# Routed experts as three f16 products of split operands, with the weights as the loaded operand

## The reference: what is computed

```
logits = xt @ gate_w.T
_, idx = top_k(logits + beta, 2)
probs = sigmoid(take_along_axis(logits, idx))
g = einsum('bh,ehm->bem', xt, gate_proj_w)      # 8 experts, 256 -> 512
u = einsum('bh,ehm->bem', xt, up_proj_w)
h = silu(g) * u
eo = einsum('bem,emh->beh', h, down_proj_w)     # 512 -> 256
combined = einsum('beh,be->bh', eo, c)          # c: probs at the two chosen experts, else 0
shared_out = the same three products with one shared expert, for every token
```

## Time and profile before

| | |
|---|---|
| median of 3 runs | 3458.92 us |
| span of the profiled execution | 3454.1 us |
| what lies around the span, by the median | 4.8 us |
| granted TensorE clock, mean | 0.982 |
| phase 1 (8 blocks) | 0 to 308 us |
| phase 2 (72 tiles) | 308 to 758 us |
| the rest | 758 to 3454 us |

### The profile page before, as it was taken

One profiled execution on the slowest core, in us unless ns is written; L12 is line 12 of the kernel. 1 busy time (PEld: TensorE's weight loads), 2 busy tenths in 40 slices (PEclk: granted clock), 3 DMA queues, 4 the chain that ended last, 5 costly groups with the idle time before them and its releaser, 6 DMA issues. The chain is left out here.

```text
span 3454.1 us, 59006 instructions
## 1 busy us (share of the span) xinstructions
PE 3251.6 (94%) x19214; PEld 1316.3 (38%) x19215; DVE 2715.8 (79%) x4886; ACT 2222.3 (64%) x3468; POOL 1600.3 (46%) x2080
## 2 busy tenths in 40 slices
PE   8998999999999999999999999778999999999987
PEld 5655666652222222222222222252334334333333
DVE  5564222559999999999999999366989999898997
ACT  3331222127888888888878888757877777777763
POOL 2124000003444343344444443306888888887885
PEclk9999999999999999999999999988999999999998
DMA  4443111111121111111111110041222222222221
GB/s 156 133 163 114 47 45 44 42 42 30 35 60 41 39 38 33 31 32 31 34 36 35 35 36 23 30 141 59 71 74 69 82 73 69 74 83 69 76 77 50
DMA packets 160884, 211.56 MB, mean 61 GB/s; under 512 B 32324, under 2 KB 108364, under 8 KB 160604
## 3 DMA queue, kind: packets, MB, share of 16 engines
q1 hardware_dynamic: 141340, 172.51, 16.6%
q0 software_dynamic: 8512, 18.76, 1.7%
q10 hardware_dynamic: 10752, 16.78, 1.5%
HBM read 154.48 MB, written 52.69 MB: 60 GB/s over the span
## 5 line engine op out<-in xcount | busy, mean ns | idle before, releaser
L1289 ACT ACTIVATE prob<-psS 128x1024 f32<-128x1024 f32 (+3 forms) x1280 | 1104.1, 906 | 275.2 <-PE psS L1473 265.6
L1339 DVE TENSOR_REDUCE pmax<-psR 128x1 f32<-128x512 f32 x1674 | 1057.0, 684 | 76.9 <-PE psR L1415 46.6
L2115 POOL TENSOR_TENSOR hc<-h_d,crep 128x512 f32<-128x512 f32 x512 | 647.3, 1272 | 187.1 <-DVE h_d L2344 136.8
L1415 PE MATMUL psR<-kslab,qslab 48*128 48x512 bf16 (+3 forms) x2480 | 651.9, 351 | 22.2 <-DVE pmax L1339 13.8
L1488 PE MATMUL psVo<-prob,vaug 128*32 128x512 f32 (+3 forms) x5120 | 627.1, 543 | 1.7 <-ACT ov L1293 0.9
L1473 PE MATMUL psS<-qslab,kslab 51*128 51x512 bf16 (+3 forms) x2560 | 531.8, 352 | 39.5 <-ACT prob L1289 24.0
L2344 DVE TENSOR_TENSOR_SCAN h_d<-a,state,psU 128x512 f32<-128x512 f32 x384 | 489.4, 1275 | 0.0
L1204 POOL TENSOR_SCALAR_AFFINE_SELECT prob<-prob 128x256 f32<-128x256 f32 (+1 forms) x512 | 213.4, 420 | 529.0 <-ACT prob L1289 529.0
L1415 PEld LDWEIGHTS psR<-kslab,qslab 48*128 48x128 bf16 x2480 | 187.3, 94 | 627.9 <-DVE pmax L1339 468.7
L2334 DVE TENSOR_TENSOR psU<-dtx,psX 128x512 f32<-128x512 f32 x512 | 356.2, 696 | 88.9 <-PE psX L2494 38.5
L2247 ACT ACTIVATE a<-dt,a_neg 128x512 f32<-128x512 f32 x512 | 366.8, 724 | 53.8 <-DVE h_d L2344 53.0
(11 more groups left out here) (309 smaller groups left out, 4805.5 us busy)
## 6 DMA issues: line engine op xcount, KB each, us to landing
crep<-c_rows_d SPq DMA_DIRECT2D x256, 256.0 KB, 3.2
x_e<-rows_d SPq DMA_DIRECT2D x72, 128.0 KB, 2.0
y_d<-y SPq DMA_DIRECT2D x72, 128.0 KB, 1.7
q_d<-parts SPq DMA_DIRECT2D x48, 128.0 KB
k_d<-parts SPq DMA_DIRECT2D x48, 128.0 KB
qslab<-q_d SPq DMA_DIRECT2D x60, 96.0 KB
kslab<-k_d SPq DMA_DIRECT2D x60, 96.0 KB
x<-in_L_attn_x_dram SPq DMA_DIRECT2D x8, 512.0 KB, 6.3
```

The lines of the kernel that those rows point to most:

```text
L1289: act.activation(prob[g % BUFS][:, :, off:BLK], psS[g % 2][:, :, off:BLK], ACT.Exp).then_inc(prob_ready, 1)
L1339: dve.tensor_reduce(into[:, lo:lo + (count - 1) * NEXT + 1:NEXT], psR[at % BANKS][:, 0:count * w].rearrange("p (n w) -> p n w", w=w), AX.X ...
L1415: ins = pe.matmul(dst[:, m * w:(m + 1) * w], qslab[u][rows, i * P:(i + 1) * P], kslab[u][rows, ch * BLK:ch * BLK + w], start=(m == 0), sto ...
L2115: pool.tensor_tensor(hc[:, g % CR], h[:, g % HR], crep[:, g // PAIR % SPR], ALU.mult).then_inc(hc_ready, 1)
```

## The change: what it does

In phase 2 each f32 product becomes three f16 products. An operand is split into a high part (the f16 nearest to it) and a low part (the rest, in f16), and high x high, low x high and high x low are added up in PSUM. For g and u the roles are exchanged: the weights, in pieces of 128 x 128, are the loaded operand, and the 128 tokens stream. So g, u and h come out with the hidden dimension on the partitions, the four transposes of h go, and h is split directly. The last product has h's parts loaded and 256 columns of weights streaming. A tile has 48 matmuls of 128 columns and 12 of 256 in place of 4 of 512, 4 of 256 and 4 transposes. psG and psU have one buffer in place of two, and the maxima three banks in place of one.

f16 has a small range, so weights are scaled by their largest magnitude. In phase 1, for each expert: its three raw matrices are loaded into one buffer `raw`; DVE takes the maximum of magnitudes over 128 x 3072 numbers (`weight_max`); PE turns the maxima (`turn_max`), DVE reduces them (`weight_row`), PE spreads them (`spread_max`), DVE computes the scales (`weight_scale`); ACT writes the high part and scales `raw` in place (`high_weights`, `scaled_weights`, six operations of 128 x 1024), and POOL subtracts to the low part (`low_weights`, three operations). Factors that undo the scales go into the silu, the product with u and the routing weights. `raw` has one buffer, so the load of expert n+1 waits for the low parts of expert n. x is now loaded where it is normalized, and `cut` has four operations in place of five.

The diff, cut to its core:

```diff
@@ phase_norm_qkv, VectorE
-                c.after(dve.tensor_tensor(rest[:], qf[:, s], parts[:, s, 0], ALU.subtract))
-                c.after(dve.tensor_copy(parts[:, s, 1], rest[:]))
-                c.after(dve.tensor_tensor(rest[:], rest[:], parts[:, s, 1], ALU.subtract))
-                dve.tensor_copy(parts[:, s, 2], rest[:]).then_inc(parts_ready[s], 1)
+                c.after(dve.tensor_tensor(qf[:, s], qf[:, s], parts[:, s, 0], ALU.subtract))
+                c.after(dve.tensor_copy(parts[:, s, 1], qf[:, s]))
+                dve.tensor_tensor(parts[:, s, 2], qf[:, s], parts[:, s, 1], ALU.subtract).then_inc(parts_ready[s], 1)
...
+            def weight_max(e):
+                dve.wait_ge(raw_in, 48 * e + 48 + CREDIT)
+                dve.tensor_reduce(wmax[:], raw[:], AX.X, ALU.max, apply_absolute_value=True).then_inc(wscale_step, 1)
...
             for n in range(NBLK):
+                weight_max(n)
                 choose(n)
                 cut(n, 0)
+                weight_row(n)
                 cut(n, 1)
                 hidden(n, 0)
                 place_rows(n)
+                weight_scale(n)
                 hidden(n, 1)
@@ phase_norm_qkv, ScalarE
             def load_expert(e):
-                act.dma_start(keep["wg"][:, e], io["gate_proj"][e].rearrange("(k p) m -> p k m", p=P))\
-                   .then_inc(keep["moe_w"], 16)
...
+                act.wait_ge(wlow_ready, 3 * e + CREDIT)
+                for w, (name, rows) in enumerate((("gate_proj", KD), ("up_proj", KD), ("down_proj", M // P))):
+                    act.dma_start(raw[:, w].rearrange("p (k m) -> p k m", k=rows),
+                                  io[name][e].rearrange("(k p) m -> p k m", p=P)).then_inc(raw_in, 16)
...
                 gate(n, 0)
                 gate(n, 1)
+                high_weights(n, 0)
+                scaled_weights(n, 0)
                 if n + 1 < NBLK:
                     token_root(n + 1)
                 copy_rows(n, 2)
+                high_weights(n, 1)
                 copy_rows(n, 3)
-                load_expert(n)
+                scaled_weights(n, 1)
                 gate(n, 2)
+                high_weights(n, 2)
                 gate(n, 3)
+                scaled_weights(n, 2)
...
                 copy_shared(n)
                 copy_values(n)
+                if n + 1 < NBLK:
+                    load_expert(n + 1)
@@ phase_norm_qkv, GpSimd
+                low_weights(n)
@@ phase_norm_qkv, TensorE
+            def turn_max(e):
+                pe.wait_ge(wscale_step, 3 * e + 1 + CREDIT)
+                pe.wait_ge(y_ready, e + CREDIT)
+                pe.transpose(psWT, wmax[:], keep["ident"][:]).then_inc(wmax_moved, 1)
...
                 product(n, "q", 0)
+                turn_max(n)
                 product(n, "q", 1)
                 product(n, "g", 0)
+                spread_max(n)
                 product(n, "u", 0)
@@ phase_experts, TensorE
+            def step(i, s):
+                if known(i + 1, 0):
+                    turn_x(i + 1, 1 - s)
                 if known(i, 0):
                     e = pe.value_load(at(keep["table"][0:1, 0], i), min_val=0, max_val=E - 1)
...
-                        for k in range(KD):
-                            ins = pe.matmul(dst[:, s], xT[:, s, k], w[:, bass.ds(e, 1), k].rearrange("p o m -> p (o m)"),
-                                            start=(k == 0), stop=(k == KD - 1))
+                        for m in range(MT):
+                            cols = slice(m * P, (m + 1) * P)
+                            for k in range(KD):
+                                w_high, w_low = (keep[w + part][:, bass.ds(e, 1), k, cols].rearrange("p o m -> p (o m)")
+                                                 for part in "hl")
+                                pe.matmul(dst[:, cols], w_high, xTh[:, s, k], start=(k == 0), stop=False)
+                                pe.matmul(dst[:, cols], w_high, xTl[:, s, k], start=False, stop=False)
+                                ins = pe.matmul(dst[:, cols], w_low, xTh[:, s, k], start=False, stop=(k == KD - 1))
...
-                if known(i - 1, 0):
-                    pe.wait_ge(h_ready, i + CREDIT)
-                    if known(i - 1, 1):
-                        pe.wait_ge(hT_ready, i - 1 + CREDIT)
-                    for m in range(MT):
-                        ins = pe.transpose(psH[:, m], h[:, 1 - s, m * P:(m + 1) * P], keep["ident"][:])
-                    ins.then_inc(h_turned, 1)
@@ phase_experts, VectorE
+                if known(i - 1, 0):
+                    dve.wait_ge(hTh_ready, i + CREDIT)
+                    dve.tensor_tensor(hTl[:, 1 - s].rearrange("p m t -> p (m t)"), h[:, 1 - s],
+                                      hTh[:, 1 - s].rearrange("p m t -> p (m t)"), ALU.subtract).then_inc(hTl_ready, 1)
```

More of the change, by code:

```diff
@@ L54 @@
 TT = NT + RT
+W_TOP = 2048.0
+X_TOP = 1024.0
 def credited(ctx, nc, sems, name):
@@ L571, in rank, with spread_max @@
                           seen[:, 0:TPB].rearrange("p j e -> p (j e)"), start=False, stop=True).then_inc(ranked, 1)
+            def turn_max(e):
+                pe.wait_ge(wscale_step, 3 * e + 1 + CREDIT)
+                pe.wait_ge(y_ready, e + CREDIT)
+                pe.transpose(psWT, wmax[:], keep["ident"][:]).then_inc(wmax_moved, 1)
+            def spread_max(e):
+                pe.wait_ge(wscale_step, 3 * e + 2 + CREDIT)
+                pe.matmul(psWB, ones[0:3, :], diag_r[:], start=True, stop=True).then_inc(wmax_moved, 1)
             def values(n):
@@ L851, in step @@
+                    dve.scalar_tensor_tensor(out=h[:, s], in0=sg[:, s], scalar=at(fac[:, 1], i), in1=psU[:],
+                                             op0=ALU.mult, op1=ALU.mult).then_inc(h_ready, 1)
                 take_max(i, 2)
-            steps(dve, step, -1, RT + 1)
-            lc = Chain(dve, lam_step)
+                if isinstance(i, int) and i == 2:
+                    scale_outputs()
+            steps(dve, step, -1, RT)
             dve.wait_ge(lam_load, 64 + CREDIT)
             lv = lam_in[:].rearrange("p (m w) d -> p m w d", w=2)
-            lc.after(dve.tensor_tensor(lam_w[:], lv[:, :, 0], lv[:, :, 1], ALU.mult))
@@ L857, in _ @@
-            lc.after(dve.tensor_reduce(lam_s[:], lam_w[:], AX.X, ALU.add))
+            fc.after(dve.tensor_tensor(lam_w[:], lv[:, :, 0], lv[:, :, 1], ALU.mult))
+            fc.after(dve.tensor_reduce(lam_s[:], lam_w[:], AX.X, ALU.add))
         @block.tensor
         def _(pe):
-            pe.wait_ge(keep["moe_w"], 16 * 3 * E)
             def max_product(i, slot):
@@ L887, in turn_x, with split_products @@
                 ins.then_inc(x_turned, 1)
+            def split_products(dst, high, low, w_high, w_low, first, last):
+                pe.matmul(dst, high, w_high, start=first, stop=False)
+                pe.matmul(dst, high, w_low, start=False, stop=False)
+                return pe.matmul(dst, low, w_high, start=False, stop=last)
             def step(i, s):
+                if known(i + 1, 0):
+                    turn_x(i + 1, 1 - s)
                 if known(i, 0):
                     e = pe.value_load(at(keep["table"][0:1, 0], i), min_val=0, max_val=E - 1)
-                    pe.wait_ge(xT_ready, i + 1 + CREDIT)
@@ L910, in step @@
+                        ins.then_inc(done, 1)
+                max_product(i, 1)
+                if known(i - 1, 0):
+                    e = pe.value_load(at(keep["table"][0:1, 0], i - 1), min_val=0, max_val=E - 1)
+                    pe.wait_ge(hTl_ready, i + CREDIT)
+                    if known(i - 1, 1):
+                        pe.wait_ge(y_ready, i - 1 + CREDIT)
                     for m in range(MT):
-                        ins = pe.matmul(psY[:], hT[:, s, m], keep["wd"][:, bass.ds(e, 1), m].rearrange("p o d -> p (o d)"),
-                                        start=(m == 0), stop=(m == MT - 1))
+                        w_high, w_low = (keep["wd" + part][:, bass.ds(e, 1), m].rearrange("p o d -> p (o d)")
+                                         for part in "hl")
+                        ins = split_products(psY[:], hTh[:, 1 - s, m], hTl[:, 1 - s, m], w_high, w_low, m == 0, m == MT - 1)
```

269 lines of the change are left out of this document (163 added, 106 removed).

## The result

The changed kernel takes 3652.3 us (median of 4 runs, 3649.4 to 3655.2) against 3459.6 us of the kernel before on the same chip: ratio 1.0557, 95% interval 1.0542 to 1.0572, so 193 us slower. The forecast was 3585. The span of the profiled execution went from 3454.1 to 3650.4 us.

A forecast was written before the change was run, and what follows sets the result against it. PE was taken to bound both phases, by its matmuls' streaming. Span 3454.1 + 85 (phase 1) + 41 (phase 2) = 3580, with 4.8 us between span and median 3585 us; range 3515 to 3680.

The forecast's parts named there:

- the sequencer sets the step: Phase 2: PE's register instructions make a loop step 6.85 us, the engine needing 4.2; +41 us for the phase.
- the sum of waits and table blocks: Phase 2, sequencer's time besides 4.7 us of address instructions: two table blocks 1.5 us, some 4 waits of 0.12, loop's end.
- Rival A: Phase 2: the sequencer keeps ahead and the engine sets a step of 4.2 us; total 3425, chance 0.05.
- Rival D: Phase 2: loads with computed addresses cost the sequencer more; 3671 at 0.02 us each, 3845 at 0.06; chance 0.11.
- Rival C: Phase 2: the starved array falls to the lower clock, 8.3 us a step; total 3690, chance 0.09.
- the wait at the head: Phase 1, blocks 1 to 7: PE idles 8.7 us before turn_max, behind the weight loads and DVE's reduction.
- Rival B: Phase 1: the new stops are hidden, by loads landing within 3 us or other PE work; total 3515, chance 0.07.
- after it the block runs as before with small shifts: Phase 1, after u0's wait for spread_max: only small shifts in the block, with down starting 10.3 us later than before.
- The clock: Phase 1: an 8.7 us pause lowers PE's clock, and products at half speed add 1.2 us a block.
- Block 0 and the passage: Phase 1's ends: block 0 +2 us for its first loads; block 7 +3 us for POOL's work before the pads' zeros.
- the signs in phase 1: PE idle 8 us or more before the second q item, block period near 47 us, clock falling once a block.
- Those of phase 2: psG's starts 6.7 to 7.0 us apart, idle put down to "issue", register instructions 0.12 apart, DVE and ACT mostly idle.

The follow-up runs named there:

- e4: Changed kernel with phase 2's weights always those of expert 0, at constant addresses (40 address instructions a step gone): 3477.7 us.
- e7: Changed kernel with the constant expert only in phase 2's last product (8 of 40 address instructions a step gone): 3590.7 us.
- e6: Changed kernel with e3's two edits, plus PE's spread_max behind u0 and each raw load waiting only for its own third of the buffer: 3523.1 us.
- e1: Changed kernel with hidden(n, 3) ahead of cut(n, 3) on DVE: 3602.8 us.
- e9: Changed kernel with DVE's order untouched and POOL's three subtractions waiting until hidden(n, 3) is done: 3588.5 us.
- e10: Changed kernel with e6's four edits, tokens as loaded operand in phase 2, and POOL's subtractions ahead of its scatters in the last block: 3382.6 us.
- e3: Changed kernel with hidden(n, 3) ahead of cut(n, 3) and the raw-weight loads issued ahead of copy_shared(n): 3546.2 us.

## Why the prediction was right in sign and short in size

- **Phase 2, the sequencer sets the step: right.** e4 and e7 show it: 0.120 us per address instruction (0.12 in the forecast) and 4.24 us for the engine alone (4.2). The loop step was 7.00 and not 6.85, the late step 6.76 and not 6.4: the sum of waits and table blocks was 0.15 and 0.36 us too small. 44 loop steps at +1.18 and 24 late ones at +0.27 add up to 58 us; the start and the end gave 3 back. For the 0.36 us of a late step I have no row that names its parts; it stays open.
- **Rival A (the engine sets phase 2): false**, by the same rows; it is what e4 looks like. **Rival D (dearer loads): false**, the pitch is that of the kernel before. **Rival C (the lower clock in phase 2): false**, 1.00 throughout, with pauses of 0.4 to 0.7 us.
- **Phase 1, the wait at the head: right in kind, too long.** PE stopped 6.98 us in the block shown and 6.3 to 7.1 in the others, not 8.7: the loads landed 7.2 us after the logits, not 8.7. The reduction was right (3.35 against 3.4). Rival B (hidden anyway) is false in the changed kernel, and e6 shows what order it would have needed.
- **The step that failed** is the sentence "after it the block runs as before with small shifts", with which `down` was to start 10.3 us later than before. It started 16.0 us later (41.5 us after the logits against 25.6). The 10.3 held no cost of the clock and no hold; without the 3.0 and 5.3 us of these the measured shift would be 7.7, so the walk through the block, whose steps are not written out, was itself too long, and this hid a part of what was missing. I priced POOL's subtractions as POOL's own time, and had DVE in their way only as an upper bound of a few us. They cost nothing on POOL and 6.2 us on DVE in every block, because they overlap a CAST ahead of the one operation that PE waits for: 5.3 us of pause, shown by e1 and e9.
- **The clock was mis-sized.** I took 1.2 us a block for one pause. Two pauses cost 3.0 and 2.8: the lower level lasts on after the pause, over 6 us of work at half speed, which the earlier trace rows showed for 4 us and I counted too lightly. So the block cost 18.3 and not 11.5.
- **Block 0 and the passage.** Block 0 was to cost 2 us, since it has no head's wait; it has the CAST like every block and cost 9 us, the other 3 came ahead of its logits. Block 7 and the passage cost 18.7 where 14.5 were forecast. POOL's work is in it, as forecast, but through DVE too: the tables stand behind the held CAST, and where nothing holds this CAST (e9) the subtractions hold the tables instead, for a gain of only 1.1 us.
- The sum: 141 + 55 = 196 us where I had 85 + 41 = 126. My bounds for phase 1 ended at 110, and those for both phases together at 3629 (the +60 in it, for phase 2, is worked out nowhere). The measured 3652.3 lies in the range of 3515 to 3680 only because half of rivals C and D was added to it, and both of these were false: that part is luck. Three of the signs in phase 1 failed as well: the pause was not 8 us or more, the block was 54.1 us and not near 47, and the clock fell twice a block and not once. Those of phase 2 came true.

## What to carry to other kernels

Before instructions are given to an idle GpSimd, look at what VectorE does at the same time and what waits behind that: a short operation of VectorE can take as long as all that GpSimd has queued, and it reads as busy time, so look at the maximum length beside the median. With addresses computed at run time, count the sequencer's register instructions per step like streamed columns (0.12 us here) and choose the roles of the operands so that one address serves the longest stream; here that alone turned a loss of 55 us into a gain of 94. New work for a queue is often free in total and dear in place: three edits of order and one finer wait took back 129 us of the change's cost without removing an operation.

## What the runs showed of the hardware that I had not expected

- DVE's CAST (f32 to bf16, both in SBUF) and its subtraction with two operands in SBUF are held by POOL's subtractions, up to 6.9 and 7.1 us for 0.42 and 0.69 in the changed kernel, over all three that follow each other. A small one is held too (128x8, 2.12 us for 0.17, e9), there for one subtraction at a time. A DVE operation with one operand in PSUM is not held (0.69 us beside POOL, e1 and e10).
- 48 pairs of load and product of 128 columns in f16 keep 56 ns each in a steady stream, and the sequencer feeds them when their addresses are constant (e4).
- A register instruction that makes an address costs PE's sequencer the same 0.12 us everywhere it was the bound: 0.119 in g and u with 128 f16 columns behind it, 0.120 in the last product with 256.
- After a pause of 7 us in f32 work PE runs at the lower of its two clock levels (granted 0.5 to 0.6 in the rows above) for some 6 us more of work; a pause of 2 us ahead of `spread_max` in e3 cost 1.7 us in one of the products behind it (3.66 us for 1.96) in some blocks and nothing in others.
